# A state-space block with a feed-forward layer: a ring of 20 C rows in the scan, turns of x one z group later in the first stage, and dt's two parts added on VectorE

## What is computed

```python
xn = (x - mu) * rsqrt(var + 1e-05) * ln_gamma + ln_beta      # of an already normalized x
xz = xn @ W_in.T                                             # 512 -> 2 x 1024
x_ssm, z = xz[..., :1024], xz[..., 1024:]
x_ssm = silu(conv4(x_ssm) + conv_b)                          # 4 taps along the sequence
xp = x_ssm @ W_xproj.T                                       # 33 columns: 1 + 16 (B) + 16 (C)
dt = softplus(xp @ W_dt.T + b_dt) + 0.001
def step(h, inp):                                            # h: 1024 channels x 16 states
    dA = exp(A * dt_t)
    dB = (1.0 - dA) / (A + 1e-08) * B_t
    h = clip(dA * h + dB * x_t, -10.0, 10.0)
    return h, sum(C_t * h, -1) + D_param * x_t
y = ys * silu(z)
x = x + y @ W_out.T
# then: norm, a gate over 7 experts, a shared and an expert product, residual
```

## Time and profile before

| | us |
|---|---|
| median of 3 runs | 4684.94 (4679.14 to 4690.98) |
| the profiled execution, its own time | 4684.51 |
| its span in the trace | 4682.7 |
| first TensorE group of the front to the end of its last store | about 94 to 1132 |
| scan, first to last step of VectorE | 1165 to 3710 |
| ffn's steady part | 3781 to 4683 |
| busy over the span: PE, DVE, ACT, POOL | 91%, 79%, 68%, 70% |

### The profile page before, as it was taken

The page is one execution under the profiler, slowest core; times in us unless marked ns, Lnnn a source line. Parts: engine busy times, 40 slices in busy tenths (PEclk is TensorE's granted clock), DMA queues, the critical chain, the costliest instruction groups (busy, mean ns, idle before and its releaser), DMA issues. The chain is left out here.

```text
span 4682.7 us, 48765 instructions
## 1 busy us (share of the span) xinstructions
PE 4279.3 (91%) x14186; PEld 2517.8 (54%) x14186; DVE 3716.3 (79%) x4288; ACT 3178.3 (68%) x5820; POOL 3285.3 (70%) x1676
## 2 busy tenths in 40 slices
PE   2999999995999999999999999999999759999999
PEld 1777777773444444444444444444444337777777
DVE  5888888884999999999999999999999744444443
ACT  1655666654999999999999999999999611211111
POOL 0233323222889999999999999999999757777772
PEclk9999999997999999999999999999999879999999
DMA  5565556665566556656655665566556444545550
GB/s 182 188 201 184 199 184 195 195 201 183 150 185 172 155 161 185 169 156 167 187 161 149 174 187 160 151 182 188 159 152 184 135 150 153 161 154 164 168 158 31
DMA packets 591700, 786.65 MB, mean 168 GB/s; under 512 B 129712, under 2 KB 332848, under 8 KB 573512
## 3 DMA queue, kind: packets, MB, share of 16 engines
q1 hardware_dynamic: 580872, 762.56, 54.6%
q10 hardware_dynamic: 10560, 20.97, 1.2%
HBM read 540.17 MB, written 245.18 MB: 168 GB/s over the span
## 5 line engine op out<-in xcount | busy, mean ns | idle before, releaser
L1091 DVE TENSOR_TENSOR_SCAN g<-dd,carry,ps_a 128x512 f32<-128x512 f32 x2048 | 2408.9, 1272 | 157.2 <-ACT dd L964 122.9
L953 POOL TENSOR_TENSOR q<-g,cc 128x1024 f32<-128x1024 f32 x1024 | 2379.6, 2385 | 205.7 <-DMA cc<-c_d 125.1
L1031 PE MATMUL ps_y<-q,w_s 128*128 128x512 f32 x4096 | 2210.5, 622 | 128.0 <-POOL q L953 127.3
L1020 PE MATMUL ps_d<-dm,xk 99*128 99x512 f32 x2048 | 1570.1, 768 | 49.0 <-DMA dm<-band_d 39.8
L975 ACT ACTIVATE ps_a<-dt_s,small 128x512 f32<-128x512 f32 x2048 | 1475.7, 721 | 5.4 <-DVE g L1091 5.4
L964 ACT ACTIVATE dd<-ps_d 128x512 f32<-128x512 f32 x2048 | 1265.9, 619 | 197.4 <-PE ps_d L1020 185.2
L1031 PEld LDWEIGHTS ps_y<-q,w_s 128*128 128x128 f32 x4096 | 719.8, 193 | 847.1 <-POOL q L953 503.4
L1020 PEld LDWEIGHTS ps_d<-dm,xk 99*128 99x128 f32 x2048 | 393.7, 193 | 653.8 <-issue 412.9
L517 PE MATMUL ps_r_f<-xnt_hi,w_hi 128*128 128x512 f32 x1024 | 431.8, 422 | 13.8 <-DVE w_lo L683 13.8
L354 POOL TENSOR_TENSOR xnt_lo<-xnt_f,xnt_hi 128x512 fp32r<-128x512 f32 x64 | 85.2, 1331 | 478.8 <-ACT xnt_hi L392 478.8
L517 PE MATMUL ps_r_f<-xnt_lo,w_hi 128*128 128x512 f32 x1024 | 410.1, 400 | 0.0
(11 more groups left out here) (160 smaller groups left out, 4407.5 us busy)
## 6 DMA issues: line engine op xcount, KB each, us to landing
w_s<-w_d SPq DMA_DIRECT2D x128, 1024.0 KB, 5.2
xk<-xt_d SPq DMA_DIRECT2D x768, 132.0 KB
xt_d<-xt_f SPq DMA_DIRECT2D x256, 256.0 KB, 3.1
cc<-c_d SPq DMA_DIRECT2D x128, 512.0 KB, 11.5
dm<-band_d SPq DMA_DIRECT2D x192, 264.0 KB
xs_d<-xs_f SPq DMA_DIRECT2D x128, 256.0 KB, 2.7
zs_d<-zs_f SPq DMA_DIRECT2D x128, 256.0 KB, 2.6
dt_d<-lg_f SPq DMA_DIRECT2D x32, 1024.0 KB, 4.4
```

The lines of the kernel that those rows point to most:

```text
L953: pool.tensor_tensor(q[:, s % QB:s % QB + 2, :], g[:, s % GB:s % GB + 2, :], cc[:, n:n + 2, :], ALU.mult).then_inc(s_q, 2)
L1020: pe.matmul(ps_d[:, i % 2, :], xk[:, (2 * blk + i // HALF) % XB, i % HALF, :], dm[:, i, :, :].rearrange("p t n -> p (t n)"), start=True, s ...
L1031: pe.matmul(ps_y[:, blk % 2, :], w[:, blk % 2, n * P:(n + 1) * P], q[:, s % QB, :], start=(n == 0), stop=(n == NS - 1)).then_inc(s_n, 1)
L1091: dve.tensor_tensor_scan(g[:, s % GB, :], dd[:, m % 2, n, :], ps_a[:, s % AB, :], carry[:, m, n:n + 1], ALU.add, ALU.mult).then_inc(s_g, 1)
```

## The change

Scan: the tile cc becomes a ring of 20 rows (10 pairs). Pair number 8 ch + i goes to slot (8 ch + i) mod 10, so the first two pairs of a chunk go where the last two pairs of the chunk before the last stood, and are loaded in blocks 3 and 4 of the chunk before; the other six are loaded in its last block, none in the first block of the new chunk. The room comes from w, which holds three half blocks instead of four, and xk, three half blocks instead of four. `load_x(blk + 2, h)` is now issued one block before its use, and the second half of w in the second half of a block. `b_ahead` is read from a small packed tensor ba_d, which two DMAs (`gather_ahead`) write once before the scan starts, and SyncE waits for these two.

Front: `turn_xs(ch, 0)` to `turn_xs(ch, 3)` follow z groups 1 to 4 instead of 0 to 3, and rows 6 and 7 of xp come right behind rows 4 and 5. VectorE does `add_positive`, as two instructions of 128x2048, behind the convolutions 6 and 7 of the next chunk; GpSimd does none of it. Both dt stores are issued together behind `store_turned(ch, 3)`. Three semaphores are merged into others.

```diff
@@ front, SyncE
                     store_xs(ch, 1)
+                    store_xs(ch, 2)
+                    store_xs(ch, 3)
+                    store_zs(ch, 0)
+                    for m in range(4):
+                        store_xs(ch, m + 4)
+                        store_zs(ch, m + 1)
+                        store_turned(ch, m)
                     if ch > 0:
                         store_dt(ch - 1, 0)
-                    store_xs(ch, 2)
-                    store_xs(ch, 3)
-                    if ch > 0:
                         store_dt(ch - 1, 1)
-                    for m in range(4):
-                        store_zs(ch, m)
-                        store_xs(ch, m + 4)
-                        store_turned(ch, m)
-                    store_zs(ch, 4)
                     store_rows(ch)
@@ front, GpSimd
                 for ch in range(CHUNKS):
-                    if ch > 0:
-                        add_positive(ch - 1, 0)
                     inverse_spread(ch + 1)
-                    if ch > 0:
-                        add_positive(ch - 1, 1)
                     rest_of_xnt(ch + 1)
@@ front, ScalarE
                     silu_x(ch, 3)
+                    silu_z(ch, 0)
                     for m in range(4):
...
+                        silu_x(ch, 4 + m)
+                        silu_z(ch, m + 1)
+                        upper_turned(ch, m)
@@ front, TensorE
+                    project(ch, "z", 0)
                     for m in range(4):
-                        project(ch, "z", m)
+                        project(ch, "z", m + 1)
                         turn_xs(ch, m)
...
-                    project(ch, "z", 4)
                     project_rows(ch, 6)
@@ front, VectorE
+                def add_positive(ch, h):
+                    dve.wait_ge(s_ln, ch * 2 + h + 1)
+                    dve.wait_ge(s_v, ch * MD + (h + 1) * XHALF)
+                    part = slice(h * XHALF, (h + 1) * XHALF)
+                    dve.tensor_tensor(lg[:, part, :], lg[:, part, :], v[:, part, :], ALU.add).then_inc(s_dt, XHALF)
...
@@ scan
-    XB, DTB, CN = 4, 3, 2
+    XB, DTB, CN, WB, CR = 3, 3, 2, 3, 10
...
-        w = sb("w_s", [P, 2, NS * P], c=c)
+        w = sb("w_s", [P, WB, NS * P // 2], c=c)
-        cc = sb("cc", [P, NS, CH], c=c)
+        cc = sb("cc", [P, CN * CR, CH], c=c)
@@ scan, SyncE
+                        pair = ch * (NS // CN) + i
+                        slot, old = pair % CR, pair - CR
+                        if old >= 0:
+                            sp.wait_ge(s_q, multiplied(STEPS * (old // (NS // CN) + 1) - NS + CN * (old % (NS // CN) + 1)))
...
+                    sp.dma_start(b_ahead[:, :], ba_d[ch // NCH, ch % NCH, :].partition_broadcast(P)).then_inc(s_ba, 16)
+
+                def gather_ahead(b):
+                    sp.dma_start(ba_d[b, :, :], xp_d[b, 1:1 + NS, 0:LEN].rearrange("n (k t) -> k n t", t=CH)[:, :, 0],
                                  allow_slow_non_contiguous=True).then_inc(s_ba, 16)
...
+                for b in range(BATCH):
+                    gather_ahead(b)
+                sp.wait_ge(s_ba, 16 * BATCH)
...
                     sp.wait_ge(s_dps, made)
-                    load_x(blk + 2, 1)
+                    load_x(blk + 2, 0)
...
-                    load_x(blk + 3, 0)
+                    load_x(blk + 2, 1)
```

More of the change, by code:

```diff
@@ L73, in build @@
             front(nc, sb, sem, t_in, ident, ones, minus_half, margin, within, clips, xs_d, dt_d, zs_d, xp_d, xt_d, bt_d, c_d)
-        scan(nc, sb, sem, ident, clips, xs_d, dt_d, xp_d, xt_d, bt_d, band_d, c_d, w_d, y_d)
+        scan(nc, sb, sem, ident, clips, xs_d, dt_d, xp_d, xt_d, bt_d, band_d, c_d, w_d, y_d, ba_d)
         ffn(nc, sb, sem, t_in, ident, minus_half, xs_d, zs_d, xp_d, w_d, y_d, out)
@@ L355, in rest_of_xnt @@
                                                ALU.subtract).then_inc(s_xl, 1)
-                def add_positive(ch, h):
-                    pool.wait_ge(s_ln, ch * 2 + h + 1)
-                    pool.wait_ge(s_v, ch * MD + (h + 1) * XHALF)
-                    for m in range(h * XHALF, (h + 1) * XHALF):
-                        pool.tensor_tensor(lg[:, m, :], lg[:, m, :], v[:, m, :], ALU.add).then_inc(s_dt, 1)
                 inverse_spread(0)
@@ L366, in _ @@
                 for ch in range(CHUNKS):
-                    if ch > 0:
-                        add_positive(ch - 1, 0)
                     inverse_spread(ch + 1)
-                    if ch > 0:
-                        add_positive(ch - 1, 1)
                     rest_of_xnt(ch + 1)
-                for h in range(2):
-                    add_positive(CHUNKS - 1, h)
             @block.scalar
@@ L458, in _ @@
                     else:
-                        act.wait_ge(s_wdl, 1)
+                        act.wait_ge(s_lo, 3)
                     keep_z(ch, 3)
@@ L743, in _ @@
                     dve.wait_ge(s_in, ch * 3 + 3)
+                for h in range(2):
+                    add_positive(CHUNKS - 1, h)
                 dve.tensor_reduce(inside1[:, :], within[:, :, :], AX.XY, ALU.min).then_inc(s_fl, 1)
@@ L747, in _, with scan @@
                 dve.wait_ge(s_fl, 3)
-def scan(nc, sb, sem, ident, clips, xs_d, dt_d, xp_d, xt_d, bt_d, band_d, c_d, w_d, y_d):
+def scan(nc, sb, sem, ident, clips, xs_d, dt_d, xp_d, xt_d, bt_d, band_d, c_d, w_d, y_d, ba_d):
     STEPS = MD * NS
@@ L785, in scan @@
         s_dm = [S(f"dm{i}") for i in range(PIECES)]
-        s_xk, s_cc = [S(f"xk{i}") for i in range(XB)], [S(f"cc{i}") for i in range(NS // CN)]
+        s_xk, s_cc = [S(f"xk{i}") for i in range(XB)], [S(f"cc{i}") for i in range(CR)]
         s_dtl = [S(f"dt{i}") for i in range(DTB)]
-        s_wl, s_xp, s_yo = ([S(f"{n}{e}") for e in range(2)] for n in ("w", "xp", "yo"))
+        s_xp, s_yo = ([S(f"{n}{e}") for e in range(2)] for n in ("xp", "yo"))
+        s_wl = [S(f"w{i}") for i in range(WB)]
         s_dps, s_dd = S("dps"), S("dd")
@@ L900, in _ @@
                     if m == 0:
-                        for i in range(4 if ch == 0 else 6, 8):
+                        for i in range(4 if ch == 0 else 8, 8):
                             load_c(ch, i)
@@ L947, in _ @@
                     ch, n = s // STEPS, s % NS
+                    pair = ch * (NS // CN) + n // CN
                     if s % STEPS < NS:
-                        pool.wait_ge(s_cc[n // CN], ch * 16 + 16)
+                        pool.wait_ge(s_cc[pair % CR], 16 * (pair // CR) + 16)
+                    rows = cc[:, CN * (pair % CR):CN * (pair % CR) + CN, :]
                     pool.wait_ge(s_g, s + 2)
```

84 lines of the change are left out of this document (42 added, 42 removed).

## The result

The changed kernel takes 4500.7 us (median; 4498.6 to 4509.5) beside 4685.1 for the kernel before, a ratio of 0.961 (95% interval 0.959 to 0.963). The forecast was 4508. The profiled execution took 4499.2, with a span of 4497.4.

The account below looks back on a forecast made before the run. VectorE bounds the scan inside chunks, late C rows its edges; TensorE bounds the front, with waits for silu. 132 - 10 + 3 + 48 + 4 = 177 us off 4684.5 gives 4508; range 4480 to 4562.

Parts of the forecast that it names:

- C ring and b_ahead: Scan, changes of chunk: GpSimd's wait for the fifth C pair and the catching up behind it go, up to 132 us.
- each of the two edits alone nearly covers 7.22 us: Scan: packing b_ahead saves 7.24 us at the store's issue; the ring gives two pairs' lead of 4.7 us.
- What is late next: Scan, changes of chunk: x halves and second weight half have margins of 1.2 to 3.3 us; 0.7 lost each, 10 us.
- Scan start: SyncE waits once for two gathers, but C rows no longer stand behind b_ahead: 3 us won, bounds 4 lost to 8 won.
- Turns and additions: Front: later turns and additions on VectorE each remove the wait for silu; 44.4 us and 15.7 of clock falls, together 60.
- xp's chain: Front: VectorE's chain to the low part of xp delays TensorE by 0 to 1 us a chunk, taken as 0.3.
- dt's stores: Front: both stores, issued together, reach `magnitude` late; bounds 0 to 3 us a chunk, taken as 0.5.
- The price on VectorE: Front, each chunk: two additions take VectorE 4.6 us, plus 0.9 for one meeting GpSimd's 1.4 us instruction.
- GpSimd by 2.3: Front: by the skill's port rule, weighed against the change, an addition on VectorE could block GpSimd for 2.3 us.
- The queue re-formed as a wait for weights: Scan rival: TensorE waits for x or weights, 4 us a change of chunk; 50 us more, 4558; chance 0.16.
- dt's stores held ScalarE up: Front rival: ScalarE held 3 to 4 us a chunk, TensorE 2.5 with the clock; 32 us more, 4540; chance 0.10.
- Three half blocks of x are enough: Scan, the rival's opposite: three are too few, TensorE waits for x in every block, slower than before, 4724 at 20.5; chance 0.04.

Follow-up runs that it names:

- the run with the old order: Changed kernel with packed b_ahead kept, but C slots, whole weights, x halves and their order as in the kernel before: 4559.0 us.
- the run with the early gathers: Changed kernel with both gathers of b_ahead's numbers issued right behind the band's fill at the head of the scan's queue: 4502.1 us.
- the last two runs above: Changed kernel with dt's stores apart and the front storing b_ahead's numbers, without gathers: 4481.5 us; the same with x turned in the old order: 4479.8 us.

## Why the prediction was right, and where its steps were not

**C ring and b_ahead, -132 us.** Right in size: from the second block on, 2383.3 us against 2382 for 2032 steps at 1.172. Wrong in one reason: "each of the two edits alone nearly covers 7.22 us". I had taken the wait for the fifth pair as the whole cause, but it is one sign of 10 MB in a queue that also carries 6.2 us of elements. With one edit the lateness goes to whatever stands next behind: to later C pairs with the old order, to the second weight half with the elements. The sum survived since both edits are in.

**What is late next, +10 us.** Too high: 1.3 us are left in the whole scan. The margins of TensorE were nevertheless too good. At the change of chunk shown above it waits 0.89 us for the second weight half, for which I had 1.2 to spare, and 8.5 us in 10 places in all. The first row is that wait, the second the longest, the third the sum:

```profile
1440.28 1.12 PE L1045 MATMUL ps_y<-q,w_s 128*128 128x512 f32 x2 [0.89 <-DMA w_s<-w_d]
...
2041.91 1.13 PE L1045 MATMUL ps_y<-q,w_s 128*128 128x512 f32 x2 [2.64 <-DMA w_s<-w_d]
...
PE ps_y L1045 <- DMA w_s<-w_d: 8.5, 10, 2.6
```

Two of these waits reach VectorE: behind the one of 2.64 us stands its gap of 1.14 at 2043.94, and behind one of 1.02 (at 2493.29, with 1.52 for x 8 us earlier) that of 0.52 at 2495.32. The other eight, of 1.1 us at most, leave no gap. I counted that TensorE runs up to a step ahead, but charged 0.7 us a change on top of margins that I held positive; in this scan a wait under about a step (1.172 us) costs nothing. Where the missing 2 us of margin went isn't shown. The halves as such are not to blame: over 34 us around a change of chunk the DMA moved 245 GB/s with them (1412 to 1446), and 240 with whole weights (the run with the old order, 1422 to 1456). An estimate by the Trainium skill (DMA: Bandwidth & Descriptors, section Bandwidth) had been 2.0 us a change for halves; no run here shows such a cost.

**Scan start, -3 us.** The sign was wrong: +4.1, just past the end of my bounds. From SyncE's timeline of the changed kernel:

```profile
1112.81 1.17 SPq L847 DMA_DIRECT2D cc<-c_d  x2
1114.01 1.41 SPq L856 DMA_DIRECT2D ba_d<-xp_d  x2
1127.75 0.32 SPq L852 DMA_DIRECT2D b_ahead<-ba_d  x1
```

I let the gathers queue behind two C pairs. In fact SyncE stands 12.3 us (1115.42 to 1127.75), with the x half, dt and C rows of the next steps unissued behind it. The failed step is the depth of that queue: it also holds both weight halves and six pieces of x, whose issue took 16.06 us. The run with the early gathers shows that this is half of it: from the fill of the band to the second block are 66.8 us in the changed kernel, 65.9 with the early gathers, and only without them 58.4 and 55.6 (the last two runs above). In the six traces with b_ahead's elements it is 62.5 to 65.2, so the gathers cost the start a little more than the elements had.

**Turns and additions, -60 us.** The mechanism was VectorE's speed and not the turns' place. I wrote that "both remove the wait for silu". Each against the kernel before that ran beside it, the later turns alone gave 5 us, the additions alone 34 and, with dt's stores apart, 67.

**xp's chain +4.5 us, dt's stores +7.5 us.** The first was 0.7 us once; my working had left 0.3 us of slack a chunk and charged it as a cost all the same. The second was mis-sized: splitting the stores brings the front's end 12.5 us forward, so they cost 0.8 us a chunk and not 0.5. ScalarE waits at most 2.6 us, inside my 0 to 3, and TensorE sees part of it. With the stores apart the front ends 63.8 us before the old one (1110.21 to 1046.46), where I had 60 - 4.5; a chunk without waits takes 59.3 us and not 59.6. The errors nearly cancel (63.8 - 12.5 for 55.5 - 7.5), and the front came out at -51.3 for -48.

**The price on VectorE.** 4.6 us a chunk was right (2.28 each). The 0.9 for meeting GpSimd didn't come on VectorE: the 32 additions take 2307 ns in the mean, setup's took 2293. GpSimd paid. VectorE's second addition of the chunk and GpSimd's next two subtractions, in the changed kernel:

```profile
554.62 2.28 DVE L641 TENSOR_TENSOR lg_f<-lg_f,v_f 128x2048 f32<-128x2048 f32 x1
```

```profile
554.62 3.43 POOL L353 TENSOR_TENSOR xnt_lo<-xnt_f,xnt_hi 128x512 fp32r<-128x512 f32 x1 [23.32 <-ACT xnt_hi L378]
559.97 1.27 POOL L353 TENSOR_TENSOR xnt_lo<-xnt_f,xnt_hi 128x512 fp32r<-128x512 f32 x1 [1.93 <-ACT xnt_hi L378]
```

The subtraction that starts with the addition takes 3.43 us instead of 1.27: 2.16 longer, nearly the whole 2.28 of the addition; one subtraction of 3.43 or 3.44 us stands in each of the chunks up to this one. The Trainium skill (SBUF — State Buffer, Who interferes with whom) says that the first to issue has the shared ports for its whole instruction and the other is blocked. In this pair the trace agrees, though which of the two issued first it doesn't tell: both rows start at 554.62. So "GpSimd by 2.3" was the better of the two prices that I weighed. It costs nothing in time, since GpSimd has slack there (23.32 and 1.93 us idle around it).

**The rivals.** The queue re-formed as a wait for weights exactly where b_ahead stayed in elements, at 101 us and not 50. In the changed kernel it stayed under what TensorE has in hand, but for the two gaps of 1.14 and 0.52 us. dt's stores held ScalarE up, by 1.7 us a chunk rather than 3 to 4 (and by my own terms that rival's price was 15 x 2.0 = 30 us, not 32). Three half blocks of x are enough: TensorE waits for xk 10.4 us in 8 places over the scan, 4.6 of them after the start; that is small, but it is one of the signs that I had named for being wrong, as are the waits for w_s and dt_d.

**The sum.** Forecast and median lie 7 us apart, and part of that closeness is luck: against the forecast the scan was 9 us better, its start 7 worse, the front 3 better and the rest 3 better.

## What to carry to other kernels

When a wait sits behind a full queue, count everything behind the slow transfer and not only the one tile that shows the wait: two edits that each seem to cover it can both be needed. When an engine is slowed by its neighbour, taking the neighbour's work away cured it here; moving the turn alone only shifted the wait. And a store that goes late in a chunk may be worth splitting, with each half issued as soon as it is ready.
